# Up products of a transformer block as pairs of 64-row matmuls, with three shared PSUM banks and one for values

## The chip, the cores and the metric

The kernel runs on one core of one Trainium2 chip. The metric is the device time of one execution in microseconds, where lower is better. Engines are named as in the profile: PE is TensorE (PEld its weight loads), DVE is VectorE, ACT is ScalarE, POOL is GpSimd, SP is SyncE, which issues most DMAs.

## The reference

A block of a diffusion transformer on 16 images of 256 tokens and 256 channels, 16 heads of 16 channels, all in float32. Cut to what matters:

```python
c_proj = silu(c) @ W_mod + b_mod                       # six vectors per image
shift_a, scale_a, gate_a, shift_m, scale_m, gate_m = split(c_proj, 6)
qkv = modulate(_ln(x), shift_a, scale_a) @ W_qkv + b_qkv
attn_out = softmax(q @ k.T * scale) @ v                # per head
x = x + gate_a * (attn_out @ W_proj + b_proj)
q_c = _ln(x) @ W_qc + b_qc                             # cross attention
k_c, v_c = split(_ln(context) @ W_kvc + b_kvc, 2)
x = x + (softmax(q_c @ k_c.T * scale) @ v_c) @ W_cproj + b_cproj
h = gelu(modulate(_ln(x), shift_m, scale_m) @ W_mlp1 + b_mlp1)   # 256 -> 1024, the up products
x = x + gate_m * (h @ W_mlp2 + b_mlp2)                           # 1024 -> 256, the down products
```

## The kernel before

The sixteen images go through a software pipeline. Each step t has a section A and a section B. Section A scans the self attention of image t ("x") while it attends the cross attention of image t-2 ("y"); section B scans y of image t-1 while it attends x of image t. A section has 16 slots, one per head. In a slot PE does two scan matmuls (scores whose row maxima DVE reduces, L640 and L927) and two score matmuls (the scores again with the maximum folded in, L650, which ACT turns into exponentials P, L781). A scan takes 48 rows of one half of the array's 128 rows and a score 49 rows of the other half, and they are issued in turns: scan, score, scan, score.

Between slots stand the other stages. A table for each engine (PE_PLAN, ACT_PLAN, DVE_PLAN, POOL_PLAN, SP_PLAN) lists for A and B the stage, a shift that gives its image, and the slot after which it comes. Engines work strictly in that order, and wait for each other by semaphores. A name that ends in a or b is the first or second half of a stage.

Matrix products of the stages that are called columns and values (L544, L554) are done in three passes: each operand is split into a high and a low float32r part, and high x high, high x low and low x high are added up. For one half of a stage, with 256 input channels (two blocks), that makes 6 matmuls of 128 rows, 128 columns and 256 streamed elements. The up products are four stages, up0 to up3, of 2 x 6 matmuls each, 48 an image, for image t-3, and all stand in section A. ACT empties each with a gelu into HH (L734), and switches its function table before and after (ACT_TABLE_LOAD), since exponentials stand around it.

Results of stages go to shared PSUM banks, which are taken in turn in the order of PE_PLAN. NBANK is 2, so a stage waits (in take) until the stage two places before it has been emptied; the semaphore for it comes from emptied: for up stages s_HH, for v_x s_V_x, for k_x the DVE half s_lo_k_x. PSUM has eight banks: two for scans, two for scores, NPV = 2 for the products with V (pv, L596) and two shared.

Stages that matter below: T_x, T_y (transposes of the normed rows, L525), v_x, k_x, q_x (projections of x), q_y (of y), out_x (L574), pv_x3 and pv_y0 (products with V), max_y1 (maxima turned by PE). From q_y the path goes through ACT (SQ_y), twelve DMAs of SP (QS_y) and to the first scan of section B.

The lines of the tables for PE's section A before:

```python
    "A": [("up0a", -3, 0), ("up1a", -3, 0), ("up0b", -3, 0), ("up1b", -3, 0), ("pv_x3", -1, 1), ("max_y1", -2, 1),
          ("v_xa", 0, 2), ("v_xb", 0, 2), ("T_x", 1, 3), ("up2a", -3, 3), ("up2b", -3, 5), ("out_xa", -1, 5),
          ("out_xb", -1, 5), ("k_xa", 1, 7), ("k_xb", 1, 7), ("up3a", -3, 7), ("up3b", -3, 7), ("pv_y0", -2, 7),
          ("T_y", -1, 8), ("max_x0", 0, 9), ("pv_y1", -2, 9), ("q_ya", -1, 9), ("q_yb", -1, 9), ("q_xa", 1, 12),
```

and for ACT's, which is the same before and after:

```python
    "A": [("up0", -3, 0), ("up1", -3, 0), ("max_y1", -2, 2), ("v_x", 0, 2), ("T_x", 1, 3), ("up2", -3, 5),
          ("k_x", 1, 6), ("up3", -3, 7), ("T_y", -1, 7), ("q_y", -1, 9), ("max_x0", 0, 9), ("q_x", 1, 13)],
```

Of the kernel before, what the change touches and what calls it, by code (L numbers as in the profile page):

```python
# [16 lines left out]
EPS = 1e-6  # L17
SCALE = HD ** -0.5
HI, LO = 0, 1
NSCAN, NPV, NBANK = 2, 2, 2  # L20
FIRST, LAST = -1, B + 2


# [5 lines left out]
    "B": [("max_x1", 0, 0), ("c_in", 1, 1), ("max_y0", -1, 4), ("k_y", 0, 4), ("out", -3, 4)],  # L29
}  # L30
PE_PLAN = {
    "A": [("up0a", -3, 0), ("up1a", -3, 0), ("up0b", -3, 0), ("up1b", -3, 0), ("pv_x3", -1, 1), ("max_y1", -2, 1),
          ("v_xa", 0, 2), ("v_xb", 0, 2), ("T_x", 1, 3), ("up2a", -3, 3), ("up2b", -3, 5), ("out_xa", -1, 5),
          ("out_xb", -1, 5), ("k_xa", 1, 7), ("k_xb", 1, 7), ("up3a", -3, 7), ("up3b", -3, 7), ("pv_y0", -2, 7),
          ("T_y", -1, 8), ("max_x0", 0, 9), ("pv_y1", -2, 9), ("q_ya", -1, 9), ("q_yb", -1, 9), ("q_xa", 1, 12),
          ("q_xb", 1, 13), ("pv_y2", -2, 14)],
    "B": [("pv_y3", -2, 0), ("max_x1", 0, 0), ("v_ya", -1, 1), ("v_yb", -1, 1), ("down0a", -3, 1), ("down0b", -3, 3),
# [21 lines left out]
}  # L59
BANKED = {"up0", "up1", "up2", "up3", "max_x0", "max_x1", "max_y0", "max_y1", "out_x", "out_y", "T_c", "T_y", "T_x",  # L60
          "T_m", "k_x", "q_x", "k_y", "q_y", "v_x", "v_y", "down0", "down1"}
HALVED = BANKED - {"T_c", "T_y", "T_x", "T_m", "max_x0", "max_x1", "max_y0", "max_y1"}


# [4 lines left out]
def counts():  # L69

    use, scans, scores, groups, n = {}, {}, {}, {}, [0, 0, 0, 0]
    filled = []
    for t in range(FIRST, LAST + 1):
        for letter, scan, attend in (("A", ("x", t), ("y", t - 2)), ("B", ("y", t - 1), ("x", t))):
            if within(scan[1]):
                scans[scan] = n[1]
                n[1] += NH
            if within(attend[1]):
                scores[attend] = n[2]
                n[2] += NH  # L80
            for name, shift, _ in PE_PLAN[letter]:
                if not within(t + shift):
                    continue
                stage = name[:-1] if name[:-1] in HALVED else name
                if stage in BANKED and name[-1] != "b":
                    use[stage, t + shift] = n[0]
                    n[0] += 1
                if stage in BANKED and name[-1] != "a":
                    filled.append(use[stage, t + shift])
                if name[:2] == "pv":  # L90
                    assert n[3] == scores[name[3], t + shift] // 4 + int(name[4])
                    groups[name, t + shift] = n[3]
                    n[3] += 1
    assert filled == list(range(n[0]))
    return use, scans, scores, groups
# [6 lines left out]
def build(nc, x, ctx_in, cond, bias, rows_in, bv_rows, wm1, wm2, wqk, wvx, wqc, wkvc, wo, wup, wdown, out):  # L102
# [8 lines left out]
    with es:  # L111
# [3 lines left out]
        def sem(name):  # L115
            return es.enter_context(nc.semaphore(name))
# [110 lines left out]
        s_MT = {s: [sem(f"s_MT_{s}{i}") for i in range(2)] for s in "xy"}  # L227
        s_HH = sem("s_HH")

        s_scan_full, s_scan_done = sem("s_scan_full"), sem("s_scan_done")  # L230
        s_score_full, s_exp = sem("s_score_full"), sem("s_exp")
        s_pv, s_pt, s_rc, s_pn, s_OT = sem("s_pv"), sem("s_pt"), sem("s_rc"), sem("s_pn"), sem("s_OT")
# [260 lines left out]
        def _(pe):  # L493
# [45 lines left out]
            def columns(w, k, blk, b, i, to):  # L539
# [7 lines left out]
                        n += 1  # L547
                return last

            def values(w, c0, k, b, a, to):  # L550
                n = 0
                for c in range(CB):
# [34 lines left out]
            def weighted(s, grp, b):  # L587
# [15 lines left out]
                **{f"pv_{s}{g}": lambda b, s=s, g=g: weighted(s, g, b) for s in "xy" for g in range(4)},  # L603
                **{f"max_{s}{h}": lambda b, s=s, h=h: maxima(s, h, b) for s in "xy" for h in range(2)},
                **{f"T_{k}": lambda b, k=k: transposes(f"T_{k}", k, b) for k in "xycm"},
                **halves("up0", lambda b, i, to: columns(w_up, "m", 0, b, i, to)),
                **halves("up1", lambda b, i, to: columns(w_up, "m", 2, b, i, to)),
                **halves("up2", lambda b, i, to: columns(w_up, "m", 4, b, i, to)),
                **halves("up3", lambda b, i, to: columns(w_up, "m", 6, b, i, to)),
                **halves("q_x", lambda b, i, to: columns(w_qk, "x", 0, b, i, to)),  # L610
                **halves("k_x", lambda b, i, to: columns(w_qk, "x", 2, b, i, to)),
                **halves("q_y", lambda b, i, to: columns(w_qc, "y", 0, b, i, to)),
# [432 lines left out]
```

## Time and profile before

| | before |
|---|---|
| median of 3 runs | 980.63 us (976.08 to 981.22) |
| span of the profiled execution, which is its own time from first to last instruction | 980.9 us |
| PE busy | 897.5 us, 91% |
| DVE, ACT, POOL busy | 63%, 60%, 35% |
| share of PE in the chain that ended last | 76% |
| mean granted clock of PE | 0.934 |

A share of busy time says how long an engine was at work over the whole span. The chain that ended last says which work the end of the program hangs on. The rows of the trace give times in us from the start of the span.

### The profile page before, as it was taken

Reading aid. Unit: us, or ns where it says so; the run is one execution under the profiler, and the core shown is the slowest. Engines: PE = TensorE matmul, PEld = TensorE weight load, DVE = VectorE, ACT = ScalarE, POOL = GpSimd, SP = SyncE. Lnnn points to the kernel's source line nnn. Section 1 sums busy time; section 2 is a strip of 40 time slices with the busy share of each in tenths; the row PEclk is TensorE's granted clock in tenths of the full one; section 3 lists DMA queues with packets and bytes.
Section 4 is the critical chain, followed back from the end, with each engine's and each line's share of the span. In section 5 each row is a group of like instructions: output and inputs, shape, how many; then the busy total and the mean of one; then the engine's idle time right before and its main releaser. Section 6 shows DMA issues by size and latency. Waiting matters only on the chain.

```text
span 980.9 us, 19308 instructions
## 1 busy us (share of the span) xinstructions
PE 897.5 (91%) x7216; PEld 657.4 (67%) x7216; DVE 617.9 (63%) x1302; ACT 590.5 (60%) x1058; POOL 348.2 (35%) x398
## 2 busy tenths in 40 slices
PE   5487899999999999999999999999999999997967
PEld 4355566677776767676777767677777767665736
DVE  3437678767767776767767767577677776644220
ACT  2142556849585767667594948567684958482522
POOL 4604044326161615253342616153433524120212
PEclk9668789999999999999999979899999999798779
DMA  7774635363445363534436333735436361130001
GB/s 214 150 101 73 105 68 107 74 86 78 91 85 86 71 116 66 107 79 82 83 82 93 80 74 74 112 67 91 92 75 88 70 90 43 34 55 33 23 0 33
DMA packets 77311, 79.21 MB, mean 81 GB/s; under 512 B 9729, under 2 KB 71810, under 8 KB 76834
## 3 DMA queue, kind: packets, MB, share of 16 engines
q1 hardware_dynamic: 76930, 77.43, 42.3%
q8 instruction: 58, 0.95, 0.5%
q10 hardware_dynamic: 288, 0.54, 0.1%
q14 instruction: 35, 0.29, 0.1%
HBM read 22.82 MB, written 4.26 MB: 28 GB/s over the span
## 4 chain that ended last, share of the span: by engine, by line
PE 76%; DVE 6%; ACT 4%; DMA 4%; SPq 4%; issue 4%; POOL 2%; POOLq 0%; ACTq 0%; DVEq 0%
PE bank L544 18%; PE scan L640 14%; PE pv L596 12%; PE bank L583 11%; PE bank L554 6%; PE bank L574 5%; PE score L650 4%; PE bank L525 3%; SPq L322 3%; DVE MX_y L927 2%; PE bank L563 2%; DMA QS_y<-SQ_y 2%; ACT P L781 2%; DVE MX_x L927 1%; DMA QS_x<-SQ_x 1%
## 5 line engine op out<-in xcount | busy, mean ns | idle before, releaser
L781 ACT ACTIVATE P<-score 128x512 f32<-128x512 f32 x512 | 289.0, 595 | 202.2 <-PE score L650 197.9
L927 DVE TENSOR_REDUCE MX_y<-scan 128x2 fp32r<-128x512 f32 x256 | 168.3, 681 | 83.2 <-PE scan L640 82.8
L927 DVE TENSOR_REDUCE MX_x<-scan 128x2 fp32r<-128x512 f32 x256 | 170.8, 679 | 78.0 <-PE scan L640 78.0
L640 PE MATMUL scan<-KS_x,QS_x 48*128 48x256 f32 x512 | 121.4, 336 | 25.8 <-DVE MX_x L927 16.2
L467 POOL TENSOR_TENSOR y<-y,x_bias 128x256 f32<-128x256 f32 x32 | 23.3, 728 | 329.7 <-DVE y L895 329.7
L544 PE MATMUL bank<-xT_y,W 128*128 128x256 f32 x960 | 136.1, 292 | 2.3 <-DVE xT_y L835 1.7
L544 PEld LDWEIGHTS bank<-xT_y,W 128*128 128x128 f32 x960 | 121.8, 194 | 14.2 <-DVE xT_y L835 6.9
L583 PE MATMUL bank<-w_down,HH 128*128 128x256 f32 x512 | 129.5, 399 | 1.0 <-ACT HH L734 1.0
L640 PE MATMUL scan<-KS_y,QS_y 48*128 48x256 f32 x512 | 111.3, 327 | 19.8 <-DMA QS_y<-SQ_y 8.0
L650 PE MATMUL score<-QS_y,KS_y 49*128 49x256 f32 x512 | 116.8, 330 | 8.1 <-ACT P L781 6.3
L640 PEld LDWEIGHTS scan<-KS_x,QS_x 48*128 48x128 f32 x512 | 76.6, 196 | 68.9 <-issue 30.3
L640 PEld LDWEIGHTS scan<-KS_y,QS_y 48*128 48x128 f32 x512 | 74.0, 195 | 69.8 <-issue 54.7
L650 PE MATMUL score<-QS_x,KS_x 49*128 49x256 f32 x512 | 111.7, 328 | 1.5 <-ACT P L781 1.5
L583 PEld LDWEIGHTS bank<-w_down,HH 128*128 128x128 f32 x512 | 96.2, 197 | 19.3 <-ACT HH L734 1.2
L650 PEld LDWEIGHTS score<-QS_y,KS_y 49*128 49x128 f32 x512 | 74.3, 193 | 17.3 <-ACT P L781 13.7
L851 DVE STREAM_TRANSPOSE PT<-pv 128x512 f32<-128x512 f32 x64 | 45.4, 710 | 63.3 <-PE pv L596 63.3
L596 PE MATMUL pv<-P,V_y 128*32 128x256 f32 x1024 | 77.1, 424 | 1.5 <-ACT P L781 1.5
L650 PEld LDWEIGHTS score<-QS_x,KS_x 49*128 49x128 f32 x512 | 73.8, 195 | 5.3 <-ACT P L781 4.1
L596 PE MATMUL pv<-P,V_x 128*32 128x256 f32 x1024 | 71.1, 397 | 0.5 <-ACT P L781 0.5
L544 PE MATMUL bank<-xT_x,W 128*128 128x256 f32 x384 | 63.0, 312 | 3.2 <-POOL xT_x L429 3.2
L544 PEld LDWEIGHTS bank<-xT_x,W 128*128 128x128 f32 x384 | 53.1, 207 | 10.1 <-POOL xT_x L429 3.6
L734 ACT ACT_TABLE_LOAD x46 | 59.0, 1283 | 0.8
(109 smaller groups left out, 1316.7 us busy)
## 6 DMA issues: line engine op xcount, KB each, us to landing
KS_x<-SK SPq DMA_DIRECT2D x96, 128.0 KB, 4.3
QS_x<-SQ_x SPq DMA_DIRECT2D x96, 128.0 KB, 4.5
KS_y<-SK SPq DMA_DIRECT2D x96, 128.0 KB, 4.4
QS_y<-SQ_y SPq DMA_DIRECT2D x192, 64.0 KB, 2.6
x_in<-in_x SPq DMA_DIRECT2D x16, 256.0 KB, 2.7
c_in<-in_ctx SPq DMA_DIRECT2D x16, 256.0 KB, 2.9
gate_a<-d_gate SPq DMA_DIRECT2D x16, 256.0 KB, 3.4
gate_m<-d_gate SPq DMA_DIRECT2D x16, 256.0 KB, 3.5
```

The source lines that it names most:

```text
L322: sp.dma_start(QS["y"][b % 2][row:row + HD, 4 * half:4 * half + 4, :].bitcast(fp32), SQ["y"][64 * half:64 * half + 64, part, par, :].bitca ...
L544: last = nc.tensor.matmul(to[:, i * N:(i + 1) * N], w[p][:, c, (blk + i) * 128:(blk + i + 1) * 128], xT[k][:, q, c, :], start=(n == 0), st ...
L554: last = nc.tensor.matmul(to[:, a * H:(a + 1) * H], xT[k][:, p, c, a * 128:(a + 1) * 128], w[q][:, c, c0:c0 + H], start=(n == 0), stop=(n ...
L574: last = nc.tensor.matmul(to[:, a * H:(a + 1) * H], OT[:, half, a * 128:(a + 1) * 128], w[:, half, :], start=(half == 0), stop=(half == 1))
L583: last = nc.tensor.matmul(to[:, 0:H], HH[:, c, a * 128:(a + 1) * 128], w_down[:, c, :], start=(c == 0), stop=(c == FB - 1))
L596: last = nc.tensor.matmul(pv_bank[half % NPV][32 * j:32 * j + 32, g * N:(g + 1) * N], V[s][:, kb, head_of(half, g, j), :], P[:, (4 * grp + ...
L640: scanned = nc.tensor.matmul(scan_bank[n % NSCAN][:, i * N:(i + 1) * N], QS[s1][b1 % 2][row:row + 3 * HD, p, i * 128:(i + 1) * 128], KS[s1 ...
L650: scored = nc.tensor.matmul(score_bank[s % 2][:, i * N:(i + 1) * N], KS[s2][b2 % 2][row:row + 3 * HD + 1, p, i * 128:(i + 1) * 128], QS[s2 ...
L734: last = nc.scalar.activation(HH[:, 2 * u + i, :], src[:, i * N:(i + 1) * N], ACT.Gelu_apprx_tanh, bias=bias_cols[:, col:col + 1])
L781: nc.scalar.activation(P[:, s % 8, :, :].rearrange("p a n -> p (a n)"), score_bank[s % 2][:, :], ACT.Exp, scale=SCALE).then_inc(s_exp, 1)
L851: nc.vector.transpose(PT[:, :, :, :].rearrange("p a b c -> p (a b c)"), pv_bank[half % NPV][:, :])\
L927: nc.vector.tensor_reduce(MX[s1][:, half, :, par, p], scan_bank[n % NSCAN][:, :].rearrange("p (a n) -> p a n", a=NB), AXIS.X, ALU.max, neg ...
```

## The change

The up products are done by pairs of 64-row matmuls. duet fills two banks at once, for up0 and up1, and again for up2 and up3. In the first burst (the a half) the upper 64 rows of the contraction of the one stage and the lower 64 rows of the other go in turns, 12 matmuls each. Then comes a slot. In the second burst (the b half) the row halves are swapped, 12 matmuls each again, and both banks are full at its end. The second burst waits on a new semaphore, s_duet, for the end of the first. In PE_PLAN up0a stands at slot 0 and up0b at slot 1, up2a at slot 3 and up2b at slot 4; up1 and up3 have no entries of their own. ACT_PLAN is unchanged. The products with V keep one bank (NPV = 1), and the shared banks become three (NBANK = 3).

```diff
-NSCAN, NPV, NBANK = 2, 2, 2
+NSCAN, NPV, NBANK = 2, 1, 3
...
-    "A": [("up0a", -3, 0), ("up1a", -3, 0), ("up0b", -3, 0), ("up1b", -3, 0), ("pv_x3", -1, 1), ("max_y1", -2, 1),
-          ("v_xa", 0, 2), ("v_xb", 0, 2), ("T_x", 1, 3), ("up2a", -3, 3), ("up2b", -3, 5), ("out_xa", -1, 5),
-          ("out_xb", -1, 5), ("k_xa", 1, 7), ("k_xb", 1, 7), ("up3a", -3, 7), ("up3b", -3, 7), ("pv_y0", -2, 7),
+    "A": [("up0a", -3, 0), ("up0b", -3, 1), ("pv_x3", -1, 1), ("max_y1", -2, 1),
+          ("v_xa", 0, 2), ("v_xb", 0, 2), ("T_x", 1, 3), ("up2a", -3, 3), ("up2b", -3, 4), ("out_xa", -1, 5),
+          ("out_xb", -1, 5), ("k_xa", 1, 7), ("k_xb", 1, 7), ("pv_y0", -2, 7),
...
+DUET = {"up0": ("up0", "up1"), "up2": ("up2", "up3")}
...
+            def duet(name, w, k, blk):
+                first, second = DUET[name]
+                def rows(to, start, lo, b, opens):
+                    n = 0
+                    for i in range(2):
+                        for c in range(CB):
+                            for p, q in PARTS:
+                                col = (start + i) * 128
+                                yield nc.tensor.matmul(to[:, i * N:(i + 1) * N], w[p][lo:lo + 64, c, col:col + 128],
+                                                       xT[k][lo:lo + 64, q, c, :], start=opens and n == 0,
+                                                       stop=not opens and n % (3 * CB) == 3 * CB - 1,
+                                                       skip_group_check=True)
+                                n += 1
+                def begin(b):
+                    pe.wait_ge(s_xT[k], b + 1)
+                    to = [take(first, b), take(second, b)]
+                    for last in zip(rows(to[0], blk, 0, b, True), rows(to[1], blk + 2, 64, b, True)):
+                        pass
+                    last[1].then_inc(s_duet, 1)
+                def end(b):
+                    to = [bank[USE[first, b] % NBANK], bank[USE[second, b] % NBANK]]
+                    pe.wait_ge(s_duet, 2 * b + (2 if name == "up2" else 1))
+                    for last in zip(rows(to[0], blk, 64, b, False), rows(to[1], blk + 2, 0, b, False)):
+                        pass
+                    last[0].then_inc(s_full, 1)
+                    last[1].then_inc(s_full, 1)
+                return {name + "a": begin, name + "b": end}
...
-                **halves("up0", lambda b, i, to: columns(w_up, "m", 0, b, i, to)),
-                **halves("up1", lambda b, i, to: columns(w_up, "m", 2, b, i, to)),
-                **halves("up2", lambda b, i, to: columns(w_up, "m", 4, b, i, to)),
-                **halves("up3", lambda b, i, to: columns(w_up, "m", 6, b, i, to)),
+                **duet("up0", w_up, "m", 0),
+                **duet("up2", w_up, "m", 4),
```

Two places show how PE's order changes. A name like bank<-xT_y,W is an up product (L544 before, L563 after), scan and score are a slot, and the semaphores that a row waits on stand in brackets. The first place is slot 0 to slot 1 of section A in a full period. Before:

```order
L640 MATMUL scan<-KS_x,QS_x 128x256
L650 MATMUL score<-QS_y,KS_y 128x256
L544 MATMUL bank<-xT_y,W 128x256 [waits s_xT_m,s_xm_m]
L544 MATMUL bank<-xT_y,W 128x256 x5
L544 MATMUL bank<-xT_y,W 128x256 [waits s_xT_m,s_y1]
L544 MATMUL bank<-xT_y,W 128x256 x5
L544 MATMUL bank<-xT_y,W 128x256 [waits s_xT_m]
L544 MATMUL bank<-xT_y,W 128x256 x5
L544 MATMUL bank<-xT_y,W 128x256 [waits s_xT_m]
L544 MATMUL bank<-xT_y,W 128x256 x5
L640 MATMUL scan<-KS_x,QS_x 128x256 [waits s_scan_done]
```

After:

```order
L674 MATMUL scan<-KS_x,QS_x 128x256
L684 MATMUL score<-QS_y,KS_y 128x256
L563 MATMUL bank<-xT_y,W 128x256 [waits s_xm_m,s_MT_y0,s_xT_m]
L563 MATMUL bank<-xT_y,W 128x256 x23
L674 MATMUL scan<-KS_x,QS_x 128x256 [waits s_scan_done]
L684 MATMUL score<-QS_y,KS_y 128x256 [waits s_exp]
L674 MATMUL scan<-KS_x,QS_x 128x256
L684 MATMUL score<-QS_y,KS_y 128x256
L563 MATMUL bank<-xT_y,W 128x256 [waits s_duet]
L563 MATMUL bank<-xT_y,W 128x256 x23
```

The 24 matmuls between slots 0 and 1 have become 24 half-height ones before slot 1 and 24 behind it, and the first burst now also takes the second bank. The second place is the end of slot 7 to T_y (the transposes of xn_y) after slot 8. Before:

```order
L544 MATMUL bank<-xT_x,W 128x256 x5
L544 MATMUL bank<-xT_y,W 128x256 [waits s_xT_m,s_x1]
L544 MATMUL bank<-xT_y,W 128x256 x5
L544 MATMUL bank<-xT_y,W 128x256 [waits s_xT_m]
L544 MATMUL bank<-xT_y,W 128x256 x5
L596 MATMUL pv<-P,V_y 32x256 [waits s_pt,s_V_y,s_exp]
L596 MATMUL pv<-P,V_y 32x256 x7
L640 MATMUL scan<-KS_x,QS_x 128x256 [waits s_scan_done,s_row_y1]
L650 MATMUL score<-QS_y,KS_y 128x256 [waits s_exp]
L640 MATMUL scan<-KS_x,QS_x 128x256
L650 MATMUL score<-QS_y,KS_y 128x256
L525 MATMUL bank<-ident,xn_y 128x128 [waits s_lo_k_x,s_xn_y]
```

After:

```order
L547 MATMUL bank<-xT_x,W 128x256 [waits s_xT_x,s_HH]
L547 MATMUL bank<-xT_x,W 128x256 x5
L547 MATMUL bank<-xT_x,W 128x256 [waits s_xT_x]
L547 MATMUL bank<-xT_x,W 128x256 x5
L632 MATMUL pv<-P,V_y 32x256 [waits s_pt,s_V_y,s_exp]
L632 MATMUL pv<-P,V_y 32x256 x7
L674 MATMUL scan<-KS_x,QS_x 128x256 [waits s_scan_done,s_row_y1]
L684 MATMUL score<-QS_y,KS_y 128x256 [waits s_exp]
L674 MATMUL scan<-KS_x,QS_x 128x256
L684 MATMUL score<-QS_y,KS_y 128x256
L528 MATMUL bank<-ident,xn_y 128x128 [waits s_HH,s_xn_y]
```

The 12 matmuls of up3 between k_x and pv_y0 (the rows of bank<-xT_y,W) are gone from here, and stand with those of up2 at slots 3 and 4. T_y no longer waits on s_lo_k_x but on s_HH, as the bank that it takes is now that of up3. k_x (bank<-xT_x,W) waits on s_HH before as well as after, for the gelu of up2, whose bank it takes in both.

## Rows read from the trace of the kernel before

**Rows 1.** The page: span, busy time by engine, and the chain that ended last.

```profile
span 980.9 us, 19308 instructions
...
PE 897.5 (91%) x7216; PEld 657.4 (67%) x7216; DVE 617.9 (63%) x1302; ACT 590.5 (60%) x1058; POOL 348.2 (35%) x398
...
PE 76%; DVE 6%; ACT 4%; DMA 4%; SPq 4%; issue 4%; POOL 2%; POOLq 0%; ACTq 0%; DVEq 0%
```

**Rows 2.** Periods by windows: busy us of each engine (count), granted clock, DMA.

```profile
455.20:509.20 54.00, 52.74 (x452) 38.65 (x450) 37.88 (x80) 36.80 (x67) 21.16 (x24) 0.97 0.45 85
509.20:561.80 52.60, 51.47 (x454) 38.13 (x452) 37.88 (x80) 36.94 (x67) 21.17 (x24) 1.00 0.49 87
561.80:618.30 56.50, 55.43 (x450) 40.17 (x450) 37.99 (x80) 36.68 (x67) 21.17 (x24) 0.91 0.39 81
618.30:674.90 56.60, 54.43 (x452) 39.99 (x450) 37.97 (x80) 36.88 (x67) 21.17 (x24) 0.94 0.47 79
```

**Rows 3.** PE in order of time, section A of one period (start, us).

```profile
487.84 3.13 PE L544 MATMUL bank<-xT_y,W 128*128 128x256 f32 x24
490.90 0.38 PE L640 MATMUL scan<-KS_x,QS_x 48*128 48x256 f32 x1
...
491.33 1.07 PE L596 MATMUL pv<-P,V_x 128*32 128x256 f32 x16
...
493.08 1.69 PE L554 MATMUL bank<-W,xT_x 128*128 128x256 f32 x12
494.70 0.38 PE L640 MATMUL scan<-KS_x,QS_x 48*128 48x256 f32 x1
...
496.43 0.38 PE L640 MATMUL scan<-KS_x,QS_x 48*128 48x256 f32 x1
...
497.10 0.98 PE L544 MATMUL bank<-xT_y,W 128*128 128x256 f32 x6
497.92 1.89 PE L574 MATMUL bank<-w_gated,OT 128*128 128x256 f32 x8
...
504.91 0.66 PE L525 MATMUL bank<-ident,xn_y 128*128 128x128 f32 x4
```

**Rows 4.** ACT in order of time, the same stretch.

```profile
490.29 1.57 ACT L734 ACTIVATE HH<-bank,bias_cols 128x256 f32<-128x256 f32 x4 [0.21 <-PE bank L544]
...
493.17 1.09 ACT L781 ACTIVATE P<-score 128x512 f32<-128x512 f32 x2
...
494.87 0.60 ACT L744 ACTIVATE V_x<-bank 128x512 f32<-128x512 f32 x1 [0.38 <-PE bank L554]
...
497.00 1.09 ACT L781 ACTIVATE P<-score 128x512 f32<-128x512 f32 x2
498.11 1.28 ACT L734 ACT_TABLE_LOAD   x1
499.40 0.84 ACT L734 ACTIVATE HH<-bank,bias_cols 128x256 f32<-128x256 f32 x2
...
502.20 0.84 ACT L726 ACTIVATE SK<-bank,bias_cols 128x256 fp32r<-128x256 f32 x2
...
504.84 0.84 ACT L734 ACTIVATE HH<-bank,bias_cols 128x256 f32<-128x256 f32 x2
```

**Rows 5.** PE in order of time: its two waits behind q_y.

```profile
510.15 0.38 PE L640 MATMUL scan<-KS_x,QS_x 48*128 48x256 f32 x1 [0.55 <-DVE MX_x L927]
...
515.64 0.35 PE L640 MATMUL scan<-KS_y,QS_y 48*128 48x256 f32 x1 [0.35 <-DMA QS_y<-SQ_y]
```

**Rows 6.** Weight loads by shape: 128 rows and 48 rows.

```profile
L544 PEld LDWEIGHTS bank<-xT_y,W 128*128 128x128 f32 x960 | 121.8, 194 | 14.2 <-DVE xT_y L835 6.9 <-issue 2.1 <-ACT HH L734 0.9
...
L640 PEld LDWEIGHTS scan<-KS_y,QS_y 48*128 48x128 f32 x512 | 74.0, 195 | 69.8 <-issue 54.7 <-DVE MX_y L927 12.7
```

**Rows 7.** DVE in order of time: the norm ahead of T_y.

```profile
503.08 0.73 DVE L828 TENSOR_SCALAR xn_y<-x,mv_y,rstd_y 128x256 f32<-128x256 f32 x2 [0.20 <-POOL rstd_y L402]
```

**Rows 8.** Windows around one fall of the granted clock (PEclk, behind POOL).

```profile
455.00:459.00 4.00, 3.32 (x26) 2.51 (x27) 3.10 (x6) 3.03 (x7) 0.00 (x0) 0.99 0.29 56
459.00:462.30 3.30, 3.30 (x24) 1.59 (x23) 0.96 (x2) 1.53 (x4) 0.00 (x0) 0.50 0.28 89
```

More of the change, by code:

```diff
@@ L84, in counts @@
                 stage = name[:-1] if name[:-1] in HALVED else name
[L85 to L89, printed above, removed]
+                for stage in DUET.get(stage, (stage,)):
+                    if stage in BANKED and name[-1] != "b":
+                        use[stage, t + shift] = n[0]
+                        n[0] += 1
+                    if stage in BANKED and name[-1] != "a":
+                        filled.append(use[stage, t + shift])
                 if name[:2] == "pv":
@@ L228, in build @@
         s_HH = sem("s_HH")
+        s_duet = sem("s_duet")
         s_scan_full, s_scan_done = sem("s_scan_full"), sem("s_scan_done")
```

## Prediction

> **What bounds the kernel now.** I read the page first. PE is busy for 897.5 of 980.9 us, and the chain that ended last runs through PE for 76% [rows 1]. So what counts is time on PE's queue, and what makes PE wait. Next I cut the trace into periods, one image each. Thirteen of them (t = 3 to 15) hold an up stage beside full sections A and B. An undisturbed period takes 52.6 us, of which PE is busy 51.5; the longer ones beside it are those where the granted clock was under 1.00 [rows 2]. Then I read one period's section A on PE in order of time [rows 3], and the same stretch on ACT [rows 4]. PE has almost no idle time there. Its first wait is 0.55 us for DVE at slot 12, its second 0.35 us for the stacked queries at the start of section B [rows 5]. ACT, only 60% busy over the span, has no gap from 497.00 to 505.68: every row there starts when the last one ends [rows 4]. That stretch decides this case.
>
> **What the row halves save.** A change of tile shape costs time. From start to start, 24 full-height matmuls take 490.90 - 487.84 = 3.06 us and 12 take 494.70 - 493.08 = 1.62, so one costs 0.12 and each stretch has 0.18 on top. For slots, one (two scan/score pairs) takes 491.33 - 490.90 = 0.43, two take 497.10 - 496.43 = 0.67: 0.12 per pair, 0.19 on top [rows 3]. A pair in opposite row halves thus costs what one 128-row matmul costs, and 48 pairs replace 48 matmuls at equal time. Saved are tile-shape changes. Slot 0, up0/up1 and slot 1 were three stretches and become one: 2 x 0.19 = 0.38 us. Around up2/up3 none is saved: the change between slot 3 and T_x stays, T_x to up2a becomes one, and up2b to out_x replaces slots to up2b. Gain: 0.4 us a period, 16 x 0.4 = 6 us in all, if nothing else moved.
>
> The Trainium skill (TensorEngine Tiling (Array Packing), Key Properties) says that changing the tiling mode drains the engine; the 0.18 to 0.19 us above agrees. The skill (TensorE: Matmul & The Clock Gate, LDWEIGHTS) also says that a load's time goes by its columns and not by its rows, which speaks against this change, since it doubles the loads. The trace agrees: 195 ns for a 48-row load, 194 for a 128-row one [rows 6]. Whether the two loads of a pair then cost double is a rival below.
>
> **What the move of up2 and up3 costs.** Both are now done by two bursts at slots 3 and 4, instead of 6 matmuls at 3, 6 at 5 and 12 at 7. ACT's plan is unchanged: gelu of up2 after the exponential of slot 5, gelu of up3 after that of slot 7. In the order of after, T_y takes the third bank behind up3, so it waits on s_HH, the gelu of up3; before, it waited on the DVE half of k_x. Before, that gelu ended at 504.84 + 0.84 = 505.68, and T_y began at 504.91 [rows 3, 4]. So even with ACT as early as now T_y would wait 0.8 us, more than the 0.4 saved. And ACT gets later. Step by step on the period of rows 3 and 4:
>
> - Slot 0 ends into 12 pairs, slot 1 into 12 more: pv_x3 starts at 490.9 instead of 491.33. Both banks are full only then, so the first gelu starts at about 491.0 instead of 490.29, +0.7.
> - The exponential of slot 1 follows four gelus and a table load of 1.28: it was done at 493.17 + 0.6 = 493.8 and is now at 494.5. Slot 3 on PE, there at 494.25, waits 0.25.
> - up2a takes two banks, and the second is that of v_x; ACT emptied it at 494.87 + 0.6 = 495.5 and does so now at about 495.7, behind two exponentials and a maximum that are 0.7 late [rows 4], PE is there at 495.5: 0.2.
> - 12 pairs, slot 4, 12 pairs, slot 5: from 495.76 that is 0.11 + 28 x 0.12 = 3.4 us, so the scores of slot 5 are full at about 499.3. ACT's exponential of slot 5 ends at 499.9; before it ended at 497.00 + 1.09 = 498.09.
> - From there ACT does table load, gelu up2, table load, exponential 6, k_x, exponential 7, table load, gelu up3: 505.68 - 498.09 = 7.6 us, gapless before and so not shorter now. The gelu of up3 ends at 499.95 + 7.6 = 507.6 [rows 4].
> - PE meanwhile: out_x, slots 6 and 7, k_x (0.4 of wait for the gelu of up2, whose bank it takes), pv_y0, slot 8: at T_y by about 505.2. It waits there 2.4 us.
>
> T_y starts at 507.6 against 504.91: +2.7 us a period, the 0.4 already taken off. Behind T_y on PE stand slot 9, max_x0, pv_y1, q_y and all that follows, and q_y starts the path through ACT and SP to the first scan of section B, which had only 0.35 us to spare on PE [rows 5]; so nothing takes the delay back. DVE's xn_y, done at 503.8 before, comes about 1.1 later with out_x, at 504.9, under the same wait [rows 7]. 13 periods x 2.7 = 35 us. The section at t = 16 has T_y too: +2. At t = 18 there are no slots between the halves, so each second burst waits for the first, and the last two gelus follow together: +1.
>
> **What the waits do to the clock.** Between 455.0 and 459.0 PE was busy only 3.32 of 4.00 us, and from 459.0 to 462.3 the granted clock was 0.50, that is 1.2 in place of 2.4 GHz [rows 8]. The period with such a stretch took 54.0 us, two with longer ones 56.5 and 56.6, against 52.6: 1.4, 3.9 and 4.0 more, 3.1 on average [rows 2]. There waits of half a us were enough sometimes (the next period has the same one at 510.15 and stayed at 1.00 [rows 2, 5]). A wait of 2.4 us in every period, with 0.25 and 0.4 shortly before it, leaves PE much emptier than that. I count on a fall in 11 of 13 periods: 11 x 3.1 = 34, less the three shown that were there already (9): +25. By the skill (TensorE: Matmul & The Clock Gate, HAM oscillation) the clock falls only for gaps of idleness longer than any that I forecast; the first row of rows 8, where the trace has no gap near that and a fall follows, speaks against it. Its result is rival B.
>
> **Small things.** One bank for values: pv_x0, pv_y0 and so on now wait for the transposition of the group before, which DVE does at least four slots earlier in its plan: 0, hidden by those slots; without this cover at most 0.7, one transposition. The wait on s_duet stands behind a slot (0.23 in mode), enough for the burst to end: 0 to 0.1.
>
> **Sum.** The profiled execution has a span of 980.9, 0.3 over the median of 980.6. 980.9 + 35 + 3 + 25 = 1044; as ACT may run a little ahead of my steps I take 1040.
>
> **Rivals.**
> - A, the forecast: wait at T_y and a low clock behind it, 1027 to 1064. 0.52.
> - B: the wait at T_y, but the clock no worse than now: 980.9 + 38 = 1019; with a wait of 1.5 instead of 2.7, which is what is left if slot 5 comes 1.2 earlier than I think, 1003. 0.28.
> - C: the two loads of a pair come one after the other in a long burst. Each pair then costs 0.24; 48 pairs x 0.12 = 5.8 us an image, all ahead of slot 5, x 16 = 92 on top of B: 1111, half of it 1065. For it speaks that a load costs the same at half the rows [rows 6], against it that four pairs in a row kept 0.12 [rows 3]; 12 in a row are not shown. 0.11.
> - D, the other side: T_y doesn't wait, because ACT's gapless stretch is not what it seems. This needs the gelu of up3 done by 504.5, 1.2 us earlier than before, though its start hangs on a slot that PE now reaches later. Then 980.9 - 6 = 975, and 965 if the disturbed periods go too. 0.05.
> - The pieces cancel, within 0.5% (about what a measurement of this kernel tells from no change): needs a delay of under 0.3 a period. 0.04.
>
> The range 1004 to 1064 holds A and B. Slower has A, B and C, 0.91.
>
> **What would show it.** In the profile after: PE idle in front of the transposes of xn_y at slot 8, released by ACT's gelu, 2 to 2.5 us in each of 13 periods; k_x released by the gelu too; no idle in front of pv for DVE; 24 64-row matmuls in 1.4 to 1.5 us; ACT without a gap between the exponential of slot 5 and the gelu of up3; a mean granted clock near 0.91 instead of 0.93. The forecast is wrong if T_y is not the wait, if the bursts take 2.8 us (C), or if the periods show no more stretches at half clock than before (B).

## The result, and the profile after

| | before | after |
|---|---|---|
| median of the runs | 980.92 us (976.08 to 984.04, 4 runs) | 1030.6 us (1027.84 to 1035.2, 4 runs) |
| span of the profiled execution | 980.9 us | 1028.4 us |
| mean granted clock in it | 0.934 | 0.932 |

The kernel is slower: the ratio of the medians is 1.0538, with an interval from 1.0493 to 1.0583. Medians, here and for the experiments, are over all runs of a kernel; the ratios leave out runs more than 1.5% above its fastest. The page of the changed kernel, in the parts that answer to [rows 1], with two groups of section 5 (busy us, mean ns, then idle time and what ended it):

```profile
span 1028.4 us, 20812 instructions
...
PE 903.8 (88%) x7984; PEld 662.1 (64%) x7984; DVE 617.5 (60%) x1302; ACT 589.8 (57%) x1058; POOL 349.2 (34%) x398
...
PE 59%; ACT 18%; issue 6%; DVE 5%; DMA 4%; SPq 4%; POOL 2%; POOLq 0%; ACTq 0%; DVEq 0%
...
L563 PE MATMUL bank<-xT_y,W 64*128 64x256 f32 x1536 | 111.1, 289 | 4.2 <-ACT V_x L778 2.5
...
L563 PEld LDWEIGHTS bank<-xT_y,W 64*128 64x128 f32 x1536 | 99.8, 191 | 9.6 <-issue 7.1
```

PE is busy 6 us more, while the span has grown by 47.5. So PE doesn't do more, it waits more, and the chain says for whom: ACT's share rose from 4% to 18%. The period that answers to [rows 3] is this one, PE in order of time (start, us; in brackets the idle time and what ended it):

```profile
506.06 1.63 PE L563 MATMUL bank<-xT_y,W 64*128 64x256 f32 x24
...
507.76 1.70 PE L563 MATMUL bank<-xT_y,W 64*128 64x256 f32 x24
509.39 1.07 PE L632 MATMUL pv<-P,V_x 128*32 128x256 f32 x16
...
512.76 0.38 PE L674 MATMUL scan<-KS_x,QS_x 48*128 48x256 f32 x1
...
513.02 0.38 PE L684 MATMUL score<-QS_y,KS_y 49*128 49x256 f32 x1
...
513.45 0.66 PE L528 MATMUL bank<-ident,xn_x 128*128 128x128 f32 x4
514.32 1.70 PE L563 MATMUL bank<-xT_y,W 64*128 64x256 f32 x24 [0.21 <-ACT V_x L778]
...
520.88 1.70 PE L547 MATMUL bank<-xT_x,W 128*128 128x256 f32 x12 [0.28 <-ACT HH L768]
...
523.73 0.28 PE L684 MATMUL score<-QS_y,KS_y 49*128 49x256 f32 x1
526.30 0.63 PE L528 MATMUL bank<-ident,xn_y 128*128 128x128 f32 x4 [2.29 <-ACT HH L768]
```

The last row is T_y. PE idles 2.29 us in front of it, until the gelu of up3 has emptied the bank. The view of one tile shows how often. Here are xn_y's rows on what ended PE's idle time in front of the transposes (us, times):

```profile
  ACT HH L768: 27.4, 12
```

Twelve waits and 27.4 us, 2.28 each. There are twelve and not thirteen full periods (t = 3 to 14): at t = 15 T_x and k_x are gone already, there being no image 16, and T_y doesn't wait for this gelu. ACT in the same stretch, answering to [rows 4]:

```profile
509.49 1.57 ACT L768 ACTIVATE HH<-bank,bias_cols 128x256 f32<-128x256 f32 x4 [1.05 <-PE bank L563]
...
512.37 1.09 ACT L815 ACTIVATE P<-score 128x512 f32<-128x512 f32 x2
...
518.08 0.60 ACT L815 ACTIVATE P<-score 128x512 f32<-128x512 f32 x1 [1.16 <-PE score L684]
518.69 1.28 ACT L768 ACT_TABLE_LOAD   x1
519.99 0.84 ACT L768 ACTIVATE HH<-bank,bias_cols 128x256 f32<-128x256 f32 x2
520.84 1.28 ACT L815 ACT_TABLE_LOAD   x1
522.14 0.60 ACT L815 ACTIVATE P<-score 128x512 f32<-128x512 f32 x1
522.67 0.84 ACT L760 ACTIVATE SK<-bank,bias_cols 128x256 fp32r<-128x256 f32 x2
523.40 0.60 ACT L815 ACTIVATE P<-score 128x512 f32<-128x512 f32 x1
524.02 1.28 ACT L768 ACT_TABLE_LOAD   x1
525.32 0.84 ACT L768 ACTIVATE HH<-bank,bias_cols 128x256 f32<-128x256 f32 x2
```

From 518.08 on every row starts when the last one ends, as before. The bank of up3 is full from about 517.8, and ACT comes to it at 525.32, since the gelu of up2, k_x, two exponentials and three table loads stand ahead of its own.

**A measure that holds in every run.** From the transposes of xn_y of section B (T_m) to those of section A (T_y) the stretch has the same length in nearly every period, because no fall of the clock lies in it. I call it the run-up. In the trace of before it goes from 479.96 to 504.91 and takes 24.95 us, after from 498.32 to 526.30 and takes 27.98:

```profile
479.96 0.66 PE L525 MATMUL bank<-ident,xn_y 128*128 128x128 f32 x4
```
```profile
498.32 0.66 PE L528 MATMUL bank<-ident,xn_y 128*128 128x128 f32 x4
```

The rest of the period, T_y to the next T_m, takes 27.6 us in both traces where it is shortest. Without a fall of the clock it reaches 28.6 before and 28.1 after, as the wait at the start of section B varies (0.35 us in [rows 5], 1.39 at 409.13). The change thus costs 3.0 us a period. It all lies in the run-up, and the experiments are read by it, beside their medians.

**Where the 47.5 us lie.** T_y of t = 3 starts at 183.71 before and at 186.39 after, that of t = 14 at 776.16 and at 809.04. So 2.7 us come at the first, 30.2 in the eleven periods behind it, and the remaining 14.6 after t = 14. Eleven run-ups give 11 x 3.03 = 33.3 by themselves; the other halves took 3.1 less than before (about 1.8 of it in the stretches with a fall of the clock, the rest in shorter waits at the start of section B). Windows of the changed kernel by period, answering to [rows 2]:

```profile
297.90:353.40 55.50, 51.59 (x498) 38.23 (x500) 37.87 (x81) 36.74 (x67) 21.19 (x25) 1.00 0.44 82
353.40:410.50 57.10, 53.19 (x498) 39.15 (x500) 37.92 (x81) 36.78 (x67) 21.23 (x25) 0.97 0.43 79
```

An undisturbed period takes 55.5 us at the shortest, against 52.6. One with a fall of the clock takes 57.1, which is 1.6 more. And this is the fall behind the wait of T_y, by windows: its last 2.5 us, 1.8 at full clock, 3.4 at half, and what follows.

```profile
523.80:526.30 2.50, 0.21 (x4) 0.03 (x2) 1.53 (x4) 2.33 (x4) 2.40 (x3) 1.00 0.67 183
526.30:528.10 1.80, 1.80 (x22) 1.10 (x26) 0.38 (x1) 1.06 (x2) 0.41 (x1) 1.00 1.17 125
528.10:531.50 3.40, 3.40 (x23) 2.59 (x16) 1.61 (x3) 1.91 (x3) 0.00 (x0) 0.50 0.77 83
```

There are seven such stretches in the twelve periods, all within 2 us of T_y and all 3.4 long, so 24 us at half clock. Before there were four between the same two points, two of them short and two long, and they made up 24 us as well. So in these runs the clock cost nothing extra in the full periods.

**The tail.** From t = 15 on the sections run out of scans, and later of slots. Waits of PE behind T_y of t = 14 (us, times, longest), the largest group of before and the same of after:

```profile
PE score L650 <- ACT P L781: 6.3, 6, 2.4
```
```profile
PE score L684 <- ACT P L815: 12.5, 10, 2.8
```

PE waits there 6.2 us more for exponentials. The longest of these waits stand behind the gelus on ACT: the one of 2.8 ends at 965.34, and ACT has done four gelus and a table load from 961.81 to 964.67 and then the exponential. At the very end, where the up products of the last image have no slots around them, PE in order of time, before and then after:

```profile
965.69 3.13 PE L544 MATMUL bank<-xT_y,W 128*128 128x256 f32 x24 [0.21 <-ACT HH L734]
969.85 7.14 PE L583 MATMUL bank<-w_down,HH 128*128 128x256 f32 x32 [1.02 <-ACT HH L734]
```
```profile
1012.20 3.46 PE L563 MATMUL bank<-xT_y,W 64*128 64x256 f32 x48 [1.02 <-ACT HH L768]
1017.40 7.14 PE L619 MATMUL bank<-w_down,HH 128*128 128x256 f32 x32 [1.75 <-ACT HH L768]
```

Both gelu waits are longer (by 0.8 and 0.7), and 24 pairs in a row take 3.46 where 24 full matmuls took 3.13. The section t = 15 to 16 also had the clock lower, by windows from T_y to T_y, before and then after:

```profile
827.70:880.20 52.50, 50.23 (x391) 35.10 (x391) 29.80 (x60) 33.37 (x60) 14.04 (x16) 0.90 0.19 42
```
```profile
862.00:921.40 59.40, 53.91 (x438) 37.97 (x438) 29.72 (x60) 33.70 (x60) 13.99 (x16) 0.83 0.17 37
```

It alone is 6.9 of the 14.6. A mean clock of 0.83 over 59.4 us means 20 us at half clock, 0.90 over 52.5 means 10.5. From T_y of t = 14 to the end it is 61 us at half clock against 48 before.

### The profile page after: what moved, and what is told of

It reads as the page before. It is cut to its first block, busy times and chain, and to the rows that moved or that the text cites. A ratio compares the mean times of both kernels' runs of the same rounds, so it can differ in the third digit from the quotient of the medians.

```text
span 1028.4 us, 20812 instructions
## 1 busy us (share of the span) xinstructions
PE 903.8 (88%) x7984; PEld 662.1 (64%) x7984; DVE 617.5 (60%) x1302; ACT 589.8 (57%) x1058; POOL 349.2 (34%) x398
## 4 chain that ended last, share of the span: by engine, by line
PE 59%; ACT 18%; issue 6%; DVE 5%; DMA 4%; SPq 4%; POOL 2%; POOLq 0%; ACTq 0%; DVEq 0%
PE bank L619 11%; PE bank L563 9%; PE pv L632 9%; PE scan L674 9%; PE bank L547 7%; ACT HH L768 5%; ACT P L815 4%; PE score L684 4%; ACT L768 4%; SPq L325 4%; PE bank L590 3%; PE bank L610 3%; DMA QS_y<-SQ_y 3%; ACT L815 2%; DVE MX_y L961 2%
## 5 line engine op out<-in xcount | busy, mean ns | idle before, releaser
L674 PE MATMUL scan<-KS_y,QS_y 48*128 48x256 f32 x512 | 109.1, 322 | 16.4 <-DMA QS_y<-SQ_y 7.3
L563 PE MATMUL bank<-xT_y,W 64*128 64x256 f32 x1536 | 111.1, 289 | 4.2 <-ACT V_x L778 2.5
L684 PE MATMUL score<-QS_x,KS_x 49*128 49x256 f32 x512 | 109.6, 323 | 1.4 <-ACT P L815 1.4
L563 PEld LDWEIGHTS bank<-xT_y,W 64*128 64x128 f32 x1536 | 99.8, 191 | 9.6 <-issue 7.1
L684 PEld LDWEIGHTS score<-QS_y,KS_y 49*128 49x128 f32 x512 | 77.0, 194 | 23.9 <-ACT P L815 15.9
L632 PE MATMUL pv<-P,V_y 128*32 128x256 f32 x1024 | 80.9, 440 | 1.2 <-ACT P L815 1.2
L768 ACT ACTIVATE HH<-bank,bias_cols 128x256 f32<-128x256 f32 x128 | 51.9, 473 | 25.8 <-PE bank L563 25.4
```

The lines of the kernel that those rows point to most:

```text
L563: yield nc.tensor.matmul(to[:, i * N:(i + 1) * N], w[p][lo:lo + 64, c, col:col + 128], xT[k][lo:lo + 64, q, c, :], start=opens and n == 0, ...
L632: last = nc.tensor.matmul(pv_bank[half % NPV][32 * j:32 * j + 32, g * N:(g + 1) * N], V[s][:, kb, head_of(half, g, j), :], P[:, (4 * grp + ...
L674: scanned = nc.tensor.matmul(scan_bank[n % NSCAN][:, i * N:(i + 1) * N], QS[s1][b1 % 2][row:row + 3 * HD, p, i * 128:(i + 1) * 128], KS[s1 ...
L684: scored = nc.tensor.matmul(score_bank[s % 2][:, i * N:(i + 1) * N], KS[s2][b2 % 2][row:row + 3 * HD + 1, p, i * 128:(i + 1) * 128], QS[s2 ...
L768: last = nc.scalar.activation(HH[:, 2 * u + i, :], src[:, i * N:(i + 1) * N], ACT.Gelu_apprx_tanh, bias=bias_cols[:, col:col + 1])
```

## The experiments

"The run-up" is the stretch from T_m to T_y, measured in a period in the middle of the trace. Ratios are against the kernel before, run on the same chip; a run stands in the order in which it was made.

| | what is changed | median us | ratio (interval) | run-up us |
|---|---|---|---|---|
| before | | 980.92 | | 24.95 |
| after | | 1030.6 | 1.0538 (1.0493 to 1.0583) | 27.98 |
| 1 | after, gelu of up3 early | 1012.05 | 1.0291 (1.0229 to 1.0353) | 25.68 |
| 2 | before, banks of after | 980.74 | 1.0009 (0.998 to 1.0037) | 24.93 |
| 3 | after, full-height matmuls | 1044.26 | 1.0674 (1.0623 to 1.0724) | 28.20 |
| 4 | duet for up0 and up1 only | 986.94 | 1.0048 (1.0015 to 1.0082) | 24.90 |
| 5 | 4, first gelus behind slot 1 | 981.94 | 0.9988 (0.9942 to 1.0034) | 24.73 |
| 6 | 1, first gelus behind slot 1 | 1005.47 | 1.0246 (1.0184 to 1.0308) | 25.62 |
| 7 | before without table loads | 970.64 | 0.9887 (0.9826 to 0.9948) | 24.94 |
| 8 | after without table loads | 986.65 | 1.0069 (1.0031 to 1.0107) | 25.66 |
| 9 | 4 without table loads | 967.89 | 0.9891 (0.9851 to 0.9931) | 24.64 |
| 10 | 7 again, beside 9 | 972.27 | 0.991 (0.9883 to 0.9937) | 24.93 |

**1. The gelu of up3 behind that of up2.** My theory: the time is lost at T_y, because ACT empties up3's bank last. So ACT does it first.

```diff
 ACT_PLAN "A":
-          ("k_x", 1, 6), ("up3", -3, 7), ("T_y", -1, 7), ("q_y", -1, 9), ("max_x0", 0, 9), ("q_x", 1, 13)],
+          ("up3", -3, 5), ("k_x", 1, 6), ("T_y", -1, 7), ("q_y", -1, 9), ("max_x0", 0, 9), ("q_x", 1, 13)],
```

> The changed kernel with one entry of ACT's table moved: the gelu of up3 directly behind that of up2, after the exponential of slot 5, in place of after slot 7. ACT then also saves one pair of table loads. Theory 1 (T_y waits for the bank of up3, which ACT empties late): the wait of 2.4 us in front of T_y shrinks to 0.2 or less, T_y starts about 2.2 us earlier, slot 9 waits up to 0.7 for the exponential of slot 7, and the time falls by 13 x 2.1 us plus some of the falls of the clock, to 990 to 1000. Theory 2 (the bursts of 64-row matmuls themselves are slow): the bursts stay as they are, the time stays within 5 us of 1030. Theory 3 (the single bank for values makes PE wait): no change either, 1030.

The profiled run had a span of 999.1. The median is 1012.05 and so outside what I gave: the other runs had mean clocks of 0.908 to 0.921 where the profiled one had 0.937. PE in order of time in one period:

```profile
503.54 1.69 PE L563 MATMUL bank<-xT_y,W 64*128 64x256 f32 x24 [0.21 <-ACT V_x L778]
...
510.10 1.70 PE L547 MATMUL bank<-xT_x,W 128*128 128x256 f32 x12 [0.28 <-ACT HH L768]
...
513.21 0.65 PE L528 MATMUL bank<-ident,xn_y 128*128 128x128 f32 x4
```

The wait at T_y is gone, and the run-up is 2.30 us shorter. This shows the cause of most of the loss. What is left, 25.68 against 24.95, stands by the rows at the two other waits for ACT that they show, and at the one at slot 3; what the bursts save is already off. T_y itself can't come earlier than this: DVE finishes xn_y at 513.15, as its row says.

```profile
512.42 0.73 DVE L862 TENSOR_SCALAR xn_y<-x,mv_y,rstd_y 128x256 f32<-128x256 f32 x2 [0.20 <-POOL rstd_y L405]
```

**2. The banks alone.** Before, with the bank numbers of after. Rival: the single values bank costs something.

```diff
-NSCAN, NPV, NBANK = 2, 2, 2
+NSCAN, NPV, NBANK = 2, 1, 3
```

> The kernel before with only the bank counts of the change: three shared banks, one for values; the up products stay full height and at their old slots. Theory 1: T_y now takes the bank of out_x, long empty, and nothing waits on the values' bank; 978 to 983, no change. Theory 3 (the single bank for values makes PE wait): pv_x0, pv_y0, pv_x2 and pv_y2 wait for a transposition, 0.7 us four times a period, up to 40 us slower, 1020.

It took 980.74, a ratio of 1.0009, with a run-up of 24.93. The banks cost nothing and give nothing.

**3. The new places with full-height matmuls.** Rival: it is the 64-row matmuls that cost the time. Here the up products stand at the places of after, but each stage is whole and full-height: up0 behind slot 0, up1 behind slot 1, up2 behind slot 3, up3 behind slot 4.

```diff
-    "A": [("up0a", -3, 0), ("up0b", -3, 1), ("pv_x3", -1, 1), ("max_y1", -2, 1),
-          ("v_xa", 0, 2), ("v_xb", 0, 2), ("T_x", 1, 3), ("up2a", -3, 3), ("up2b", -3, 4), ("out_xa", -1, 5),
+    "A": [("up0a", -3, 0), ("up0b", -3, 0), ("up1a", -3, 1), ("up1b", -3, 1), ("pv_x3", -1, 1), ("max_y1", -2, 1),
+          ("v_xa", 0, 2), ("v_xb", 0, 2), ("T_x", 1, 3), ("up2a", -3, 3), ("up2b", -3, 3), ("up3a", -3, 4), ("up3b", -3, 4), ("out_xa", -1, 5),
...
-                **duet("up0", w_up, "m", 0),
-                **duet("up2", w_up, "m", 4),
+                **halves("up0", lambda b, i, to: columns(w_up, "m", 0, b, i, to)),
+                **halves("up1", lambda b, i, to: columns(w_up, "m", 2, b, i, to)),
+                **halves("up2", lambda b, i, to: columns(w_up, "m", 4, b, i, to)),
+                **halves("up3", lambda b, i, to: columns(w_up, "m", 6, b, i, to)),
```

> The changed kernel with its banks and with the up products at the same places (up0 after slot 0, up1 after slot 1, up2 after slot 3, up3 after slot 4), but as full-height matmuls of 128 rows, 12 in each place. Theory 1 (place and bank, not the row halves): T_y still waits 2 to 2.7 us for the gelu of up3, and the saved changes of tile shape are back, 0.4 us a period, partly offset because up0 is full earlier for ACT: 1028 to 1038. Theory 2 (the row halves are slow): back to 980 to 990.

It took 1044.26, a little above the bound. PE in order of time:

```profile
523.66 1.70 PE L547 MATMUL bank<-xT_x,W 128*128 128x256 f32 x12 [0.28 <-ACT HH L770]
...
529.08 0.63 PE L528 MATMUL bank<-ident,xn_y 128*128 128x128 f32 x4 [2.29 <-ACT HH L770]
```

The same waits stand at k_x and T_y, to the hundredth. So they come from where the work stands, not from the row halves; those make the run-up 0.22 us shorter than this kernel's. The rival has fallen. The ratios of the two kernels don't overlap either; in the profiled runs the rest of the difference is mostly the clock, which this kernel had at 1.2 GHz for 44 us between 180 and 840, against 24.

**4. The duet for up0 and up1 alone.** up2 and up3 are as before; three shared banks, one for values. This isolates the gain that I had counted.

```diff
 PE_PLAN "A", against before:
-    "A": [("up0a", -3, 0), ("up1a", -3, 0), ("up0b", -3, 0), ("up1b", -3, 0), ("pv_x3", -1, 1), ("max_y1", -2, 1),
+    "A": [("up0a", -3, 0), ("up0b", -3, 1), ("pv_x3", -1, 1), ("max_y1", -2, 1),
...
-                **halves("up0", lambda b, i, to: columns(w_up, "m", 0, b, i, to)),
-                **halves("up1", lambda b, i, to: columns(w_up, "m", 2, b, i, to)),
+                **duet("up0", w_up, "m", 0),
```

> Three shared banks and one for values, the paired 64-row bursts for up0 and up1 alone; up2 and up3 are full height at the slots of the kernel before. Theory 1: PE saves 0.38 us a period, of which slot 3 and q_y give back 0.2 to 0.4, since ACT's gelus start 0.7 us later and its queue has no gaps up to the transposes: 976 to 983. Theory 2 (the row halves are slow): half of the loss of the change, 1000 to 1010.

986.94 by the median is outside again, though the profiled run had a span of 977.1; its twelve runs lie between 978.49 and 995.49. The run-up is 24.90, only 0.05 better than before. The reason is at slot 3, PE in order of time:

```profile
492.12 0.38 PE L675 MATMUL scan<-KS_x,QS_x 48*128 48x256 f32 x1
492.38 0.38 PE L685 MATMUL score<-QS_y,KS_y 49*128 49x256 f32 x1
```

The score starts 0.26 us behind its scan. Before, the scan started at 494.70 [rows 3] and the score with it:

```profile
494.71 0.38 PE L650 MATMUL score<-QS_y,KS_y 49*128 49x256 f32 x1
```

In experiment 4 it waits for a score bank, which the late exponential of slot 1 has not read yet. So the burst's gain is given back at once, on ACT.

**5. As 4, the gelus of up0 and up1 behind the exponential of slot 1.** If ACT reads slot 1 first, the bank comes free in time.

```diff
 ACT_PLAN "A":
-    "A": [("up0", -3, 0), ("up1", -3, 0), ("max_y1", -2, 2), ("v_x", 0, 2), ("T_x", 1, 3), ("up2", -3, 5),
+    "A": [("up0", -3, 1), ("up1", -3, 1), ("max_y1", -2, 2), ("v_x", 0, 2), ("T_x", 1, 3), ("up2", -3, 5),
```

> The kernel of e4_first_duet (three shared banks, paired bursts for up0 and up1 alone) with ACT's gelus of up0 and up1 moved from after slot 0 to after slot 1, where both banks become full. Theory 1 (what the bursts save is given back by ACT's exponential of slot 1, which stands behind the late gelus): slot 3 no longer waits 0.25 us for it, a period falls by 0.2 to 0.3 us against e4, and the time by 3 to 5 us at equal clock: 973 to 980, 0.3 to 0.7% below the kernel before. If ACT's order at this place does not matter, it equals e4: 977 to 987.

Scan and score of slot 3 start together again, at 498.57. The run-up is 24.73, which is 0.17 better than 4, a little less than I gave, and 0.22 better than before. Over 16 images that would be 3.5 us. The median, 981.94, is above what I gave, and its ratio of 0.9988 can't be told from no change. The mechanism is seen in the trace; as a way to make the kernel faster it is not shown.

**6. Both moves of gelus in the changed kernel** (1 and 5 together).

> The changed kernel (both pairs in bursts) with two moves in ACT's table: the gelus of up0 and up1 after slot 1, that of up3 directly behind that of up2 after slot 5. Theory 1: against e1 the waits at slot 3 (0.25) and in front of up2a (0.35) go, the wait of k_x for the gelu of up2 (0.46) stays: about 0.5 us a period less than e1, so 992 to 1005 with e1's clock, and about 0.7 us a period above the kernel before. If the remaining loss of e1 came from the row halves and not from ACT, it stays at 1001 to 1012.

The run-up is 25.62, 0.06 better than 1, where I had expected 0.5: this expectation failed. The wait at slot 3 is gone, but the rows show where it went, PE in order of time:

```profile
502.33 1.70 PE L563 MATMUL bank<-xT_y,W 64*128 64x256 f32 x24 [0.42 <-ACT V_x L778]
...
508.89 1.70 PE L547 MATMUL bank<-xT_x,W 128*128 128x256 f32 x12 [0.27 <-ACT HH L768]
```

up2a now waits 0.42 for v_x's bank where it waited 0.21 before. The four gelus and two table loads have to be done somewhere between slots 0 and 3, and PE meets ACT's lateness at one place or the next. The median of 1005.47 lies in the band that I gave for a loss from the row halves, but the run-up makes up only 12 x 0.67 = 8 us of it, and the rest lies in the clock and the tail. What is left of the run-up, 0.67, is by the rows at these two waits, and experiment 9 below shows the row halves without such waits to be faster and not slower. Against 1012.05 in experiment 1 the ratios overlap.

**7 to 10. Without table loads.** Identity stands in place of gelu in these four; they compute another function for HH, and ACT has no table to switch. (The expectation of 7 speaks of 45 loads out of 46; the traces have 92 before and one in 7.) This takes 1.28 us off ACT's queue for each switch and nothing off PE's. The edit is the same in each:

```diff
-                                                ACT.Gelu_apprx_tanh, bias=bias_cols[:, col:col + 1])
+                                                ACT.Identity, bias=bias_cols[:, col:col + 1])
```

7 is before, 8 is after, 9 is the kernel of experiment 4, and 10 is 7 again on the chip of 9.

> The kernel before with ACT's Identity in place of the gelu, which leaves out the function and with it 45 of ACT's 46 table loads (1.28 us each); the output is not that of the reference. A control for e8. PE bounds a period and has no wait for the gelus, so little changes: 970 to 981.

> The changed kernel with Identity in place of the gelu in the same way, so ACT's stretch between the exponential of slot 5 and the emptying of up3's bank is 3.8 us shorter. Theory 1 (the loss is PE's wait for ACT, and the bursts themselves save 0.38 us a period): T_y no longer waits, and the time lies 3 to 8 us below e7. Theory 2 (the row halves, or reading two banks at once, cost PE time): it stays 20 us or more above e7.

7 took 970.64, with the run-up as it was, 24.94: before, ACT's table loads cost the run-up nothing. That 7 is 1% below before lies mostly behind T_y of t = 14, where it takes 191.3 us against 204.7. For 8 my expectation failed. It took 986.65, 16 more than 7 and so between my two theories. PE and then ACT in order of time:

```profile
510.09 0.63 PE L528 MATMUL bank<-ident,xn_y 128*128 128x128 f32 x4 [0.86 <-ACT HH L768]
```
```profile
507.89 0.84 ACT L760 ACTIVATE SK<-bank,bias_cols 128x256 fp32r<-128x256 f32 x2 [1.29 <-PE bank L547]
508.62 0.60 ACT L815 ACTIVATE P<-score 128x512 f32<-128x512 f32 x1
509.10 0.85 ACT L768 ACTIVATE HH<-bank,bias_cols 128x256 f32<-128x256 f32 x2
```

T_y still waits, though ACT has time to spare now (it idles 1.29 us in front of k_x). The emptying of up3 stands in ACT_PLAN behind k_x, which PE fills late, and behind the exponential of slot 7. So the order on ACT alone leaves a wait of 0.86 us, and the run-up is 25.66 against 27.98: without the table loads 2.3 of the 3.0 us are gone. Experiment 1 took the same 2.3 away by the order, with most loads still in place. So these are not two shares that add up: late order and table loads together make the wait, and taking either away removes most of it. I had taken the gapless stretch for the whole cause, and without it a part stays. The clock is another part of the 16: nine of the periods had a fall, and their stretch from T_y to T_m took 29.0 instead of 27.6. They don't stand behind T_y but 7.7 us later, behind PE's wait of 0.54 us for the maxima of x, which the trace of before has too [rows 5]. By windows:

```profile
514.40:517.80 3.40, 2.72 (x23) 1.91 (x20) 2.77 (x6) 2.52 (x7) 0.00 (x0) 1.00 0.53 86
517.80:521.20 3.40, 3.40 (x26) 2.10 (x25) 1.29 (x2) 1.86 (x4) 0.00 (x0) 0.50 0.24 82
```

> The kernel of e4_first_duet (bursts for up0 and up1 alone, up2 and up3 full height at their old places) with Identity in place of the gelu, so without ACT's table loads; the output is not that of the reference. Here neither ACT nor the norm of y is in the way of the bursts. Theory 1 (merging three stretches of PE into one saves 0.38 us a period): the way from the transposes T_m to T_y, and slot 0 to pv_x3, is 0.3 to 0.4 us shorter a period than in e10, 4 to 6 us in all: 963 to 968. If the pairs cost more than full-height matmuls in long bursts, it is not faster than e10.

> The kernel of e7_before_no_tables once more, as the control of e9 on the same chip: 966 to 972 as before. Nothing in it changes between the theories.

9 has a run-up of 24.64 and 10 one of 24.93. The median of 10, 972.27, is a little above what I gave. With ACT out of the way the first duet saves 0.29 us a period, close to the 0.38 counted in the prediction. The medians, 967.89 and 972.27, have ratios that overlap.

## Why the prediction was right, and where it was off

**The direction and the case.** Forecast were 1040 us and slower, with a stall at T_y as the mechanism; measured were 1030.6 us and that stall. That the number lies in the band of rival A is partly luck: A's low clock behind T_y was there, but it cost no more than the falls of before, and it was the end of the program, at 14.6 us where 3 were counted, that lifted the time above the 1019 of rival B. The single steps, with the times of after moved by 18.36 us (T_m stands at 479.96 before and 498.32 after):

| step | predicted | measured |
|---|---|---|
| pv_x3 starts | 490.9 | 491.03 |
| first gelu starts | 491.0 | 491.13 |
| exponential of slot 1 done | 494.5 | 494.6 |
| wait at slot 3 | 0.25 | 0.26 |
| exponential of slot 5 done | 499.9 | 500.3 |
| from there to the gelu of up3 done | 7.6 | 7.5 |
| wait of k_x for the gelu of up2 | 0.4 | 0.28 idle |
| PE is at T_y | 505.2 | 505.6 (idle from 524.01) |
| T_y starts | 507.6 | 507.94 |
| run-up longer by | 2.7 | 3.03 |

**What the row halves save.** Right in kind and near in size. The bursts of 12 pairs last 1.63 and 1.70 us, as 12 full-height matmuls do (1.69 in [rows 3]), so a pair costs one matmul also twelve times in a row. Rival C fell with these rows. The saving is 0.29 a period by 9 and 10, where 0.38 was predicted.

**Waiting for T_y's bank.** Right: experiment 1 takes the wait away, and 2.30 of 3.03 us with it. Its cause is finer than the prediction had it. The step "gapless before and so not shorter now" holds with the table loads in place; without them (experiment 8) the stretch has gaps, and 0.7 us of the 3.0 stays from ACT's order.

**xn_y "under the same wait".** Right, but sized too small: 1.8 later than in [rows 7] and not 1.1, done at 523.95 or, moved, 505.59. With T_y's bank free it is what T_y has next (experiment 1). DVE's row in the trace of after:

```profile
523.21 0.74 DVE L862 TENSOR_SCALAR xn_y<-x,mv_y,rstd_y 128x256 f32<-128x256 f32 x2 [0.20 <-POOL rstd_y L405]
```

**Small things.** Right: experiment 2 has the banks at nothing, and no row of pv has a wait for DVE's transposition.

**The clock.** This term, +25, failed. A fall was counted at 3.1 us and in 11 of 13 periods. The mean of three falls in [rows 2] (1.4, 3.9 and 4.0) was no fair price: the long ones didn't repeat. Behind T_y's wait came seven short falls at 1.6 us each; before there were four falls between the same two points, one of them ahead of [rows 2], with as much time at half clock. The profiled run of after had a mean clock of 0.932, where about 0.91 was forecast and before had 0.934. The step "leaves PE much emptier than that" was argued and not shown: after has more falls, but not more time at half clock in the full periods, and so the size of this term was rival B's, which is nothing. The Trainium skill (TensorE: Matmul & The Clock Gate, HAM oscillation) names long gaps of idleness as what lets the clock fall. Here it did fall, to half, within 2 us of a wait of 2.29, and in experiment 8 within 3 us of one of 0.54. The rule's result was rival B, 1019 at most, and the time came out 12 above that, by the tail.

**The tail.** This term, +3, failed the other way, at 14.6. I had counted one section with T_y's wait (t = 16, +2) and one without slots (t = 18, +1). In fact T_y waits for the gelu neither at t = 15 (there is no k_x) nor at t = 16, where it waits 0.41 for xn_y, and every section from there on pays. PE waits 6.2 us more for exponentials in all; that it does so because with fewer scans it reaches each slot sooner is argued and not shown. 0.8 and 0.7 more come at the two last gelu waits. The experiments narrow the rest down. From T_y of t = 14 to the end the changed kernel takes 219.4 us and experiment 3 takes 219.1, so the row halves are not the cause. Experiments 7 and 10 are one kernel and take 191.3 us with about 20 at half clock and 199.5 with about 40. By that price, which makes it an estimate, the 13 us more at half clock of the changed kernel are 5 to 6 of the 14.6. At about equal clock 8 takes 204.0 against the 199.5 of 10, so some 4 us stay without any table load.

**The sum.** Stall in the full periods: predicted 35, measured 2.7 + 33.3 = 36, though in twelve periods of 3.0 and not thirteen of 2.7. The other halves, with the clock, and the tail: predicted 25 + 3, measured -3.1 + 14.6. Two wrong sizes of opposite sign made the forecast look closer than its parts were.

**What stays open.** Which of the possible falls happen is not settled. The wait of 2.29 us came twelve times alike and was followed by a fall seven times. The wait of about 0.54 us for the maxima of x stands in nearly every period of every kernel here; in 8 a fall followed it nine times, in the profiled run of before twice (one is in [rows 8]). Nor do I know why experiments 1 and 4 had most of their runs at a lower clock than the profiled one.

## What to carry to other kernels

Where banks are taken in turn, moving a product earlier doesn't help until the engine that empties it comes earlier too: follow each bank to its next user, and read from the emptying engine's own order what stands ahead of the emptying. If the next user is a stage that the kernel's tempo hangs on, its wait is paid in full every period. And count the sections at the ends of a pipeline one by one: what hides a delay in a full period may be missing there, and here they cost as much as the stall of five periods.

## What the runs showed of the hardware that I had not expected

- Two 64-row matmuls in opposite row halves cost as much as one of 128 rows, their two weight loads included: 1.63 to 1.70 us for 12 such pairs, at 191 ns for a load of 64 rows. In a row of 24 pairs with nothing in between a small cost showed, 3.46 us against 3.13.
- How many falls of the clock a run has does not go by the size of its longest wait: 8, whose waits are all under 1 us, had nine of them in full periods, and the changed kernel, with 2.29 us in each, seven. What it does go by is not shown. A stretch of 3.4 us at half clock cost 1.4 to 1.6 us in both.
- A table switch on ACT costs 1.28 us and no more: in the rows of after the load starts at 524.02 and the gelu at 525.32. The Trainium skill (ScalarE: Activation LUTs, What ACT_TABLE_LOAD costs) adds a drain of 1.38 us to each; the trace has no room for it.
